# Attention scores two slots earlier in a merged attention and MLP loop, with one more buffer of exponentials and of pairs

## The reference

```python
xn = _layernorm(x, axis=-1)
x = x + _L0_attn_ref(xn, Wq, Wkv, Wo, bo) + _L0_ffn_ref(xn, gate_W_packed, gate_scales, ...)
```

```python
scores = jnp.einsum('brgtd,bgsd->brgts', qg, k) / jnp.sqrt(jnp.float32(HD))
scores = jnp.where(causal[None, None, None], scores + bias[None], -jnp.inf)
attn = jax.nn.softmax(scores, axis=-1)
out = jnp.einsum('brgts,bgsd->brgtd', attn, v)
```

```python
gelu = jnp.tanh(0.7978845608028654 * (gate + 0.044715 * gate ** 3)) * gate * 0.5 + gate * 0.5
inter = gelu * up
out = jnp.einsum('tn,hn->th', inter, Wd)
```

## Time and profile before

| | us |
|---|---|
| runs, median of 3 | 1734.5 (1733.62 to 1833.09) |
| the profiled execution | 1738.0 |
| its span, first to last instruction | 1736.1 |
| loop, first MLP matmul to the next head's | head 0 starts at 118.9, head 15 at 1575.0 |

### The profile page before, as it was taken

The page is one execution under the profiler, slowest core; times in us unless marked ns, Lnnn a source line. Parts: engine busy times, 40 slices in busy tenths (PEclk is TensorE's granted clock), DMA queues, the critical chain, the costliest instruction groups (busy, mean ns, idle before and its releaser), DMA issues.

```text
span 1736.1 us, 28858 instructions
## 1 busy us (share of the span) xinstructions
PE 1476.8 (85%) x9281; PEld 710.1 (41%) x9281; DVE 1277.7 (74%) x2642; ACT 991.9 (57%) x2124; POOL 1001.2 (58%) x670
## 2 busy tenths in 40 slices
PE   6968878889888889888888898888888888998589
PEld 4743434434433434334333344444343343444234
DVE  7748767686868688686868687777858686776466
ACT  3336656566656566556666566565656565665440
POOL 3126656566656667575656567565656566665341
PEclk9989989999999999999999899999999999999889
DMA  7778758696988878686988778796879687776666
GB/s 217 218 166 171 154 95 162 133 167 128 158 153 151 149 126 167 121 162 129 165 142 154 138 139 159 123 166 122 167 136 163 133 148 150 127 143 118 119 169 203
DMA packets 781358, 260.95 MB, mean 150 GB/s; under 512 B 733408, under 2 KB 750696, under 8 KB 780664
## 3 DMA queue, kind: packets, MB, share of 16 engines
q1 hardware_dynamic: 776888, 253.48, 75.9%
q10 hardware_dynamic: 4320, 5.64, 1.1%
HBM read 52.30 MB, written 21.89 MB: 43 GB/s over the span
## 4 chain that ended last, share of the span: by engine, by line
PE 31%; DVE 16%; issue 14%; POOL 13%; DMA 10%; SPq 5%; ACT 3%; ACTq 0%; DVEq 0%; POOLq 0%
POOL pair L1706 9%; DMA pt<-pair 8%; PE gate_ps L1322 8%; PE down_ps L1300 6%; PE up_ps L1322 6%; PE o_ps L1363 5%; PE s_ps L1339 4%; POOL il L1714 3%; DVE mxp L1557 3%; DVE wf L379 2%; SPq L1177 2%; DVE acc L1514 2%; DVE prod L1538 2%; DVE dec L370 1%; DVE dec L366 1%
## 5 line engine op out<-in xcount | busy, mean ns | idle before, releaser
L1706 POOL TENSOR_TENSOR pair<-p,pair 128x1024 f16<-128x1024 f32 (+7 forms) x384 | 619.2, 1620 | 405.4 <-ACT pair L1454 404.7
L1444 ACT ACTIVATE p<-s_ps,shift 128x512 f32<-128x512 f32 (+3 forms) x640 | 394.1, 620 | 240.8 <-POOL pair L1706 165.6
L1339 PE MATMUL s_ps<-kst,qst 128*128 128x512 f32 (+3 forms) x640 | 357.0, 560 | 122.8 <-ACT p L1444 109.2
L1454 ACT ACTIVATE pair<-p 128x1024 f16<-128x1024 f32 (+7 forms) x384 | 308.0, 806 | 125.9 <-DMA pt<-pair 122.6
L1557 DVE TENSOR_REDUCE mxp<-s_ps 128x1 f32<-128x512 f32 x384 | 262.3, 684 | 101.7 <-PE s_ps L1339 101.1
L1714 POOL TENSOR_TENSOR il<-prod,ih 128x512 f16<-128x512 f32 x128 | 156.3, 1221 | 142.9 <-DVE ih L1546 142.9
L1514 DVE TENSOR_TENSOR acc<-down_ps,acc 128x512 f32<-128x512 f32 x237 | 161.8, 683 | 96.4 <-PE down_ps L1300 94.6
L1300 PE MATMUL down_ps<-wh,ih 128*128 128x512 f16 x506 | 203.7, 403 | 24.1 <-DVE acc L1514 24.1
L1339 PEld LDWEIGHTS s_ps<-kst,qst 128*128 128x128 f32 x640 | 127.6, 200 | 232.2 <-ACT p L1444 143.3
L1363 PE MATMUL o_ps<-pt,vst 128*32 128x256 f16 (+1 forms) x3456 | 136.2, 298 | 84.1 <-DMA pt<-pair 83.0
L1322 PE MATMUL gate_ps<-xh,wh 128*128 128x512 f16 x512 | 203.7, 398 | 0.0
(11 more groups left out here) (252 smaller groups left out, 2091.0 us busy)
## 6 DMA issues: line engine op xcount, KB each, us to landing
o<-oraw SPq DMA_DIRECT2D x256, 64.0 KB, 2.1
qst<-q_parts SPq DMA_DIRECT2D x192, 64.0 KB
q_parts<-o SPq DMA_DIRECT2D x24, 256.0 KB, 3.4
pt<-pair SPq DMA_TRANSPOSE x384, 4.3
raw<-L_ffn_gate_W_packed_dram SPq DMA_DIRECT2D x16, 256.0 KB, 3.8
raw<-n_L_ffn_up_W_packed_dram SPq DMA_DIRECT2D x16, 256.0 KB, 3.6
raw<-L_ffn_down_W_packed_dram SPq DMA_DIRECT2D x32, 128.0 KB, 3.2
rb<-l_recips SPq DMA_DIRECT2D x16, 256.0 KB
```

The lines of the kernel that those rows point to most:

```text
L1339: nc.tensor.matmul(s_ring[n % len(s_ring)][:, 0:cols], qst[:, c, i4 * P:(i4 + 1) * P], kst[:, m * CH:m * CH + cols], start=True, stop=True ...
L1444: nc.scalar.activation(p32[p % PR][:, at:at + cols], s_ring[n % len(s_ring)][:, 0:cols], ACT.Exp, bias=shift[t % len(shift)][:, 0:1], accu ...
L1454: nc.scalar.activation(pair[n % PH][:, 0:cols], p32[n % PR][:, 0:cols], ACT.Copy).then_inc(phi_done, 1)
L1706: nc.gpsimd.tensor_tensor(pair[n % PH][:, cols:2 * cols], p32[n % PR][:, 0:cols], pair[n % PH][:, 0:cols], ALU.subtract).then_inc(plo_done, 1)
```

## The change

1. `LEAD` 6 to 8 and `VALUES_LAG` 6 to 8: blocks, exponentials, parts and transposes stand two slots earlier, value products and copies where they stood.
2. `PR` 2 to 3, `PH` 3 to 4: one more buffer of exponentials, one more pair.
3. `qst` becomes a ring of two chunks. Chunks 0 and 1 of the next head are loaded in slots 20 and 37, chunks 2 and 3 of the same head in slots 0 and 6.
4. `rb` is gone. The reciprocals go into parts 2 and 3 of the value buffer `o3`, in the halves that are free once the parts are added up. The load becomes four DMAs and waits for these sums.
5. `mask_row` is built in the preamble and stays; its zeros take the place of `zeros`; `ident` lives in the preamble only. VectorE's setup has three instructions less.
6. `LOAD_K_AT` 39 to 37.

```diff
-LEAD = 6
+LEAD = 8
-TURN_LAG, VALUES_LAG = 2, 6
+TURN_LAG, VALUES_LAG = 2, 8
-LOAD_Q_AT = {2: 0, 9: 1, 21: 2, 40: 3}
-LOAD_K_AT, LOAD_V_AT = 39, 0
+LOAD_Q_AT = {0: (0, 2), 6: (0, 3), 20: (1, 0), 37: (1, 1)}
+LOAD_K_AT, LOAD_V_AT = 37, 0
...
-            qst = tile("qst", [P, NCH, CH], F32R)
+            qst = tile("qst", [P, 2, CH], F32R)
...
+    rb = [o[:, 2:4, CH // 2:] for o in o3]
...
         sp.wait_ge(r_out, 16 * (P // TURN) * (h + 1))
-        if h:
-            sp.wait_ge(on_done, h)
-        sp.dma_start(rb[:], r_s[h % 2].rearrange("(c o t) -> c o t", o=1, t=CH).broadcast_to([NCH, HD, CH])
-                     ).then_inc(rb_in, 16)
+        sp.wait_ge(osum_done, (VPARTS - 1) * (h + 1))
+        for c in range(NCH):
+            sp.dma_start(rb[h % 2][c * HD:(c + 1) * HD],
+                         r_s[h % 2, c * CH:(c + 1) * CH].rearrange("(o a t) -> o a t", o=1, a=2).broadcast_to([HD, 2, CH // 2])
+                         ).then_inc(rb_in, 16)
...
-        nc.gpsimd.tensor_tensor(on, on, rb[:], ALU.mult).then_inc(on_done, 1)
+        nc.gpsimd.tensor_tensor(on.rearrange("p (a t) -> p a t", a=2), on.rearrange("p (a t) -> p a t", a=2), rb[h % 2], ALU.mult).then_inc(on_done, 1)
...
+        if c >= 2:
+            return
         sp.wait_ge(p_out[1], 32 * (c + 1))
...
-        PR, PH = 2, 3
+        PR, PH = 3, 4
...
-                    sp.wait_ge(block_done, (i - 1) * NBLK + TILE_END[c * TPC + TPC - 1])
-                    sp.dma_start(qst[0:AUG, c, :].bitcast(F32), aug_s[bass.ds(i * AUG, AUG), cols]).then_inc(q_in[c], 16)
+                    h, b = i - (c < 2), c % 2
+                    sp.wait_ge(block_done, h * NBLK + TILE_END[(c + 2) % NCH * TPC + TPC - 1])
+                    sp.dma_start(qst[0:AUG, b, :].bitcast(F32), aug_s[bass.ds(i * AUG, AUG), cols]).then_inc(q_in[b], 16)
...
+                        for ahead, c in [LOAD_Q_AT[s]] if s in LOAD_Q_AT else ():
+                            if i + ahead < HEADS:
+                                load_q(i + ahead, c)
                         if i < LAST:
-                            if s in LOAD_Q_AT:
-                                load_q(i + 1, LOAD_Q_AT[s])
...
-                            pe.wait_ge(q_in[c], (h + 1) * 64)
+                            pe.wait_ge(q_in[c % 2], (2 * h + c // 2 + 1) * 64)
...
-                nc.vector.memset(zeros[:], 0.0).then_inc(set_up, 1)
-                nc.vector.memset(mask_row[:, 0:CH - P], 0.0).then_inc(set_up, 1)
-                nc.vector.tensor_copy(mask_row[:, CH - P:], mask_ts[:]).then_inc(set_up, 1)
```

More of the change, by code:

```diff
@@ L203, in build @@
         acc = sb("acc", [P, NT, C], F32)
-        ident = sb("ident", [P, P], F32)
-        mask_ts = sb("mask_ts", [P, P], BF16)
+        mask_row = sb("mask_row", [P, CH], BF16)
         sc = [sb(f"sc{m}", [P, NG, SB], F32) for m in range(3)]
@@ L253, in build @@
             v_in = sem("v_in")
-            q_in = [sem(f"q_in{c}") for c in range(NCH)]
+            q_in = [sem(f"q_in{c}") for c in range(2)]
             p_out = [sem(f"p_out{j}") for j in range(1 + KVH)]
@@ L436, in preamble @@
         e[n] for n in ("x_d", "Wq", "Wkv", "scales", "augq", "augk", "q_s", "k_s", "v_s", "aug_s"))
-    xh, xl, acc, ident, mask_ts, sc, tab, oscale, vscale, oback, os_s, os_done, os_out = (
-        e[n] for n in ("xh", "xl", "acc", "ident", "mask_ts", "sc", "tab", "oscale", "vscale",
+    xh, xl, acc, mask_row, sc, tab, oscale, vscale, oback, os_s, os_done, os_out = (
+        e[n] for n in ("xh", "xl", "acc", "mask_row", "sc", "tab", "oscale", "vscale",
                        "oback", "os_s", "os_done", "os_out"))
@@ L448, in sem @@
             return ctx.enter_context(nc.semaphore(name))
+        ident = sb("ident", [P, P], F32)
         xin = [acc[:, i * TPC:(i + 1) * TPC, :] for i in range(2)]
@@ L626, in _ @@
                 nc.gpsimd.memset(ident[:], 0.0).then_inc(pool_step, 1)
[L627 removed]
+                nc.gpsimd.memset(mask_row[:], 0.0).then_inc(pool_step, 1)
                 pool.wait_ge(pool_step, 2)
@@ L630, in _ @@
                                         pattern=[[-1, P]], channel_multiplier=1).then_inc(ident_done, 1)
-                nc.gpsimd.affine_select(out=mask_ts[:], in_=mask_ts[:], compare_op=ALU.is_ge, fill=-1e30, base=0,
+                nc.gpsimd.affine_select(out=mask_row[:, CH - P:], in_=mask_row[:, CH - P:], compare_op=ALU.is_ge, fill=-1e30, base=0,
                                         pattern=[[-1, P]], channel_multiplier=1).then_inc(pool_step, 1)
@@ L973, in main_loop @@
     x_d, out_d, bo, raw, dec, wf, sc = (e[n] for n in ("x_d", "out_d", "bo", "raw", "dec", "wf", "sc"))
-    xh, xl, acc, mask_ts, tab, oback = (
-        e[n] for n in ("xh", "xl", "acc", "mask_ts", "tab", "oback"))
+    xh, xl, acc, mask_row, tab, oback = (
+        e[n] for n in ("xh", "xl", "acc", "mask_row", "tab", "oback"))
     wh, wl, cur, qst, kst, vst, o3 = (
@@ L1151, in load_q @@
                     cols = slice(c * CH, (c + 1) * CH)
-                    sp.wait_ge(block_done, (i - 1) * NBLK + TILE_END[c * TPC + TPC - 1])
-                    sp.dma_start(qst[0:AUG, c, :].bitcast(F32), aug_s[bass.ds(i * AUG, AUG), cols]).then_inc(q_in[c], 16)
+                    h, b = i - (c < 2), c % 2
+                    sp.wait_ge(block_done, h * NBLK + TILE_END[(c + 2) % NCH * TPC + TPC - 1])
+                    sp.dma_start(qst[0:AUG, b, :].bitcast(F32), aug_s[bass.ds(i * AUG, AUG), cols]).then_inc(q_in[b], 16)
                     for part, at in ((0, HD), (1, 2 * HD), (0, 3 * HD)):
-                        sp.dma_start(qst[at:at + HD, c, :].bitcast(F32), q_s[part, bass.ds(i * HD, HD), cols]).then_inc(q_in[c], 16)
+                        sp.dma_start(qst[at:at + HD, b, :].bitcast(F32), q_s[part, bass.ds(i * HD, HD), cols]).then_inc(q_in[b], 16)
                 for seeded in SEEDED:
@@ L1338, in block @@
                         cols = columns(t, m)
-                        nc.tensor.matmul(s_ring[n % len(s_ring)][:, 0:cols], qst[:, c, i4 * P:(i4 + 1) * P],
+                        nc.tensor.matmul(s_ring[n % len(s_ring)][:, 0:cols], qst[:, c % 2, i4 * P:(i4 + 1) * P],
                                          kst[:, m * CH:m * CH + cols], start=True, stop=True).then_inc(block_done, 1)
@@ L1358, in values @@
                                 if u == 0 and len(todo) == VPARTS - 1:
-                                    todo.append((zeros[:], rows, 0))
+                                    todo.append((mask_row[:, 0:HD].bitcast(F16), rows, 0))
                         for k, (lhs, rhs, tok) in enumerate(todo):
@@ L1387, in project @@
                         mm.then_inc(y_done, 1)
-                pe.wait_ge(set_up, 6)
+                pe.wait_ge(set_up, 3)
                 pe.wait_ge(square_done, after(0))
@@ L1487, in wo_high @@
                     nc.scalar.activation(woh[:, g, :], wo[g], ACT.Copy, scale=wscale).then_inc(wo_hi, 1)
-                act.wait_ge(set_up, 6)
+                act.wait_ge(set_up, 3)
                 loop(act, body)
```

11 lines of the change are left out of this document (4 added, 7 removed).

## The result

The kernel after takes 1658.3 us (median of four, 1655.7 to 1660.4) where the kernel before takes 1739.3: a ratio of 0.954, 95% interval 0.950 to 0.959. One of the four runs of the kernel before took 1833.1 us, a slow one; the median counts it, the ratio leaves it out. The forecast was 1640 us. The profiled execution took 1660.4 us (span 1658.6) against 1738.0: 77.5 us less, where 94.5 were forecast.

The account below looks back on a forecast made before the run. TensorE, idle 12.5 us a head in waits and slowed behind them, bounds the kernel; -7.0 us a head over fourteen heads (-98), with first head, last head and tail, gives -94.5: 1640 us from 1734.5, range 1615 to 1675 (chance 0.50).

Parts of the forecast that it names:

- The sum by stretches: Whole kernel: fourteen ordinary heads at -7.0 us each, -98; last head -4; first -4, +5 and +1.5; tail +5.
- The value products: TensorE's waits at slot 47 (3.2 us) and slot 13 (0.8 us) go: -4.0 us a head.
- The block waits: Score blocks waiting for exponentials: 6.8 to 5.4 us a head, with 2.8 at slot 12, 1.2 at 23, 0.8 at 33.
- rival B: GpSimd's lower halves collide with VectorE's decoding: +8.6 us a head, 1760 us; in full or C 0.15, B or D partly 0.12.
- The clock: Slow matmuls behind TensorE's waits: -1.9 at slot 47, -1.0 at slot 35, +0.6 at slot 14, together -2.3 us a head.
- The buffers: Third exponentials' buffer and fourth pair: zero by themselves, upper bound another -0.6 us a head.
- ScalarE's waits for transposes are nearly gone: Sign that the forecast holds: ScalarE, which waited 6.7 us a head for a pair buffer, hardly waits there any more.
- Reciprocals: Four DMAs for one at slot 11: 1.2 us more of SyncE, hidden by its waits, so cost nothing.
- Queries: Chunks 2 and 3 loaded at slots 0 and 6: +0.3 us a head, between 0 and +2; first head +5.
- The tail: End of the kernel: the spread of reciprocals waits for the last sum, +2 to +8 us, taken as +5.
- A: Rival: waits behind decoding fall too, block waits 5.4 to 1.4, 77 us more gained, 1563 us; chance 0.14.
- C: Rival: SyncE, in order, keeps its waits, so no gain, 1735 to 1740 us; chance with B in full 0.15.
- D: Rival: query chunk 2 late in every head, 7 us each, 1770 us; chance with more B collisions 0.09.

Follow-up runs that it names:

- lead_only: The kernel before with `LEAD` and `VALUES_LAG` at 8 and the keys at slot 37, buffers, queries and `rb` as before: 1740.3 us, ratio 1.002.
- lead_7: The kernel after with `LEAD` and `VALUES_LAG` 7, keys at slot 38, query chunks at slots 1, 7, 21 and 38: 1691.7 us, ratio 0.974.
- all_three: The kernel after with keys at slot 35, last reciprocals in an exponentials' buffer without waiting for sums, head 0's third query chunk loaded earlier: 1636.6 us, ratio 0.941.

## Why the prediction was right, and where it was not

The direction, the places and most of the size were right: 1640 forecast, 1658 measured, inside the likeliest case's own range. That the number came so close is in part luck. The prediction gave the whole gain to the distance and nothing to the buffers and the reciprocals. The distance alone gains nothing (`lead_only`, 1.002), with the rest of the change but the buffers it gains 1.5%, and only with the fourth pair some 5%; the pair was in the change for a reason that the sum did not have. The time lost at the keys, which it did not see either, is most of the 18 us by which the measured time lies above the forecast.

**The sum by stretches.** Heads 1 to 14 went from 1357.0 us (218.0 to 1575.0) to 1275.0 (219.2 to 1494.2): -82.0, against -98. Head 0 and its start added 1.2, against 2.5. From head 15 to the end of the span it took 164.4 for 161.1: +3.3, against +1. Together -77.5.

**The value products** (-4.0 a head): right. Their waits fell by 43.1 us in eleven heads, 3.9 a head. `lead_only` shows that the distance does this.

**The block waits** (6.8 to 5.4): the sum came to 6.6, and the places were partly wrong. At slot 12, idle is 0.4 instead of the 2.8 forecast: the copy `cur` ahead of the decoding there takes 0.58 us as a mean for 1.75 before. At slot 2 it is 0.7, for which there was no term. At slot 16 it is 1.7 instead of 0.3. VectorE in the head at 675.3, and GpSimd beside it:

```profile
699.75 0.69 DVE L380 TENSOR_TENSOR wf<-dec,sc 128x512 f32<-128x512 f16 x1
...
701.41 2.12 POOL L1706 TENSOR_TENSOR pair<-p,pair 128x1024 f16<-128x1024 f32 x1
701.55 2.54 DVE L380 TENSOR_TENSOR wf<-dec,sc 128x512 f32<-128x512 f16 x1
704.01 0.55 DVE L1562 CUSTOM_DVE_ANT_0 s_ps<-s_ps,mask_row 128x384 f32<-128x384 f32 x1
```

The same multiplication takes 0.69 and 2.54 us, the second ahead of the `shift` at 704.85 for which the exponential of block 18 waits, and with it block 22. It is so in all eleven heads: the multiplication starts 0.13 us after a lower half of GpSimd has begun and ends 0.55 us after that has ended. The 44 multiplications that took less than 0.8 us all started while GpSimd was idle. So rival B's mechanism is there, but a collision moved rather than was added: as means, step 370 fell from 1.47 to 1.24 us (B's sign was that it would grow), the multiplications took 1.02 for 0.98, the cast `ih` 0.86 for 0.57, and VectorE in all 809.5 us for 807.7. The Trainium skill (SBUF — State Buffer, Who interferes with whom) calls the port pair of VectorE and GpSimd an exclusive lock for an instruction's length; this trace agrees with it in kind. At slots 19, 23 and 33 idle is 0.5, 1.6 and 1.5 (forecast 0.1, 1.2 and 0.8).

**The clock** (-2.3 a head): the size was nearly right, busy time fell by 2.85, and the reason was incomplete. I had expected slow stretches to stay behind slots 12, 23 and 33. In the ordinary heads none stayed. The eight at value products went with these waits, as forecast; the 16 at blocks went though the block waits kept their sum, now in six waits a head (67 / 11) of at most 1.85 us. That the splitting did this is read from the two traces; no run changed the splitting alone, and in `lead_7`, where 19.0 of 22.3 us are busy time, seven of the stretches are at value products.

**The keys** (no term at all): the step that failed, and the largest miss to the slow side. The prediction listed the move from slot 39 to 37 and costed the queries and the transposes, but never asked what stands on SyncE ahead of the keys once the transposes have moved by two slots as well. Three heads of 99.3 instead of 88.6 us are 32 us, of which 14 come back by moving the load. The forecast for an ordinary head, 89.5, was within 1 us of the 88.6 measured. With the load moved the kernel takes 1644.7 us, 5 above the forecast instead of 18.

**The buffers** (zero, upper bound -0.6 a head): wrong by most of the gain. The fourth pair is worth 3.0 to 3.5%. The prediction took the blocks and the upper halves to keep their distance to the transposes when all move together. But not all of SyncE's work moves: gathers and turned weights keep their slots, and with three pairs the next upper half waits for a transpose behind them. `lead_only` shows the price: the block waits rise by 37.8 us in eleven heads. The sign "ScalarE's waits for transposes are nearly gone" came only by half, 38.4 us for 73.9:

```profile
ACT pair L1457 <- DMA pt<-pair: 38.4, 21, 4.0
```

The third buffer of exponentials is indeed worth nothing; ScalarE's waits for lower halves (123.3) were the harmless ones.

**Reciprocals** (zero): wrong. The price of the three added issues was right (1.3 us for 1.2), but the 256 KB transfer held the transpose behind it, and that is gone: 17 us, measured beside three pairs. The row with the maximum of 4928 ns said that such a transpose was there.

**Queries** (+0.3 a head; head 0 +5): right. They wait 0.8 us in eleven heads, and block 12 of head 0 waits 6.9.

**The tail** (+5): right in kind. GpSimd waits 7.72 us for the spread, and `all_three` took 5.3 us out.

```profile
1623.61 1.84 POOL L324 TENSOR_TENSOR o<-o 128x512 f32<-128x512 f32 x1 [7.72 <-DMA o<-l_recips]
```

**The rivals.** A did not come: the block waits behind the decoding stayed. C named the right engine for `lead_only` and for the keys, where SyncE's order costs; for the kernel as a whole it is refuted, SyncE's waits for lower halves fell from 222.0 to 169.8 us. Its sum counted twice: the 1.78 us of a transpose have the wait for the lower half in them. The Trainium skill (Perfetto Trace Analysis, Identifying the Most-Contended Engine) would have the most-contended engine optimised first. I had read this as "no less work, no gain", and it does not say that: no engine's work became less (VectorE 1277.7 us before, 1286.3 after), and the 4.6% came out of idle time and slow clock on TensorE, the busiest row before and after (85% and 86%). D did not come, except in head 0. The 217 value products of a head are 216; nothing hangs on it.

## What to carry over

When one stage is moved against others that share an in-order queue, ask of each ring between them whether its buffers are held longer: here the pairs needed one more and the exponentials did not. Look at the length of each wait, not only at their sum: here the block waits kept their sum in shorter pieces, and the slow stretches behind them went. And follow each rare load (here one head in four) along its in-order queue after the move: what was ahead of it has changed too.

## What the runs showed of the hardware

- The transpose issued right behind one transfer of 256 KB into 128 partitions kept SyncE for 4.5 to 4.9 us, each time, whether its lower half came 1.0 or 2.6 us after the start; behind four of 64 KB it took 2.0 to 2.2 as a mean. That it is the issue that is held, and not only the landing, I had not expected.
- In the eleven heads of the kernel after, no stretch at 1.2 GHz began at one of the ordinary waits of up to 1.85 us, and the granted share was 0.50 behind the key wait of 7.88 us. The length of the one wait does not settle it: in the kernel before it was 0.50 behind 1.61 us, 0.59 behind 2.19 us and 1.00 behind 2.78 us (keys).
- The same VectorE multiplication took 0.69 us when it began with GpSimd idle and 2.54 when it began 0.13 us into a GpSimd instruction of 2.12 us; then it ended 0.55 us after that one, eleven times of eleven.
